# An AdaLN block with a selective scan and 16 experts on one core: ScalarE and VectorE get own moments for single stages

## The reference, cut to what matters

```
h = layernorm(x) * (1 + ca) + sa                      # ca, sa ... : one set of six vectors per row
x = x + ga * ssm(h)
h = layernorm(x) * (1 + cb) + sb
x = x + gb * moe(h)

ssm(x): xn = norm(x); xb, z = split(xn @ W_in)        # 512 channels each
        xb = silu(conv3(xb)); dt = softplus(xb @ W_dt + b_dt)
        B, C = xb @ W_B, xb @ W_C                     # 16 states
        h_t = exp(dt_t * A) * h_(t-1) + dt_t * x_t * B_t ; y_t = sum_n h_t C_t   # scan over the tokens
        y = (y + D * xb) * silu(z) ; return x + y @ W_out
moe(x): scores = sigmoid(x @ gate.T); choose 2 of 4 groups, then 4 of 16 experts; weights normalised
        y = sum_e weight_e * down_e(silu(gate_e x) * up_e x)                     # all 16 are computed
```

## Time and profile before

| | |
|---|---|
| median of three runs | 2831.57 us |
| profiled execution | 2827.36 us, its span 2825.6 us |
| busy | PE 85%, PEld 60%, DVE 86%, ACT 55%, POOL 79% |
| mean granted TensorE clock | 0.926 of full |
| DMA moved | 626.19 MB, mean 222 GB/s |

### The profile page before, as it was taken

The page is one execution under the profiler, slowest core; times in us unless marked ns, Lnnn a source line. Parts: engine busy times, 40 slices in busy tenths (PEclk is TensorE's granted clock), DMA queues, the critical chain, the costliest instruction groups (busy, mean ns, idle before and its releaser), DMA issues.

```text
span 2825.6 us, 29196 instructions
## 1 busy us (share of the span) xinstructions
PE 2398.6 (85%) x9004; PEld 1685.0 (60%) x9004; DVE 2430.4 (86%) x2482; ACT 1564.0 (55%) x2945; POOL 2237.5 (79%) x1563
## 2 busy tenths in 40 slices
PE   3445698989989898997989899898989989898899
PEld 1212466666756666675666667566666756666678
DVE  2678899989989898999989899998989899898932
ACT  3555665556556556656665665566566556655311
POOL 1577888888888888888888888888888888887922
PEclk7667899999989899999999899998989999899999
DMA  4699899999999999999999999999999999998921
GB/s 111 180 225 232 227 235 242 231 235 237 239 234 231 234 228 237 236 239 234 236 241 232 232 238 235 234 234 234 238 232 235 237 233 237 231 241 220 258 70 49
DMA packets 354510, 626.19 MB, mean 222 GB/s; under 512 B 51488, under 2 KB 162080, under 8 KB 354352
## 3 DMA queue, kind: packets, MB, share of 16 engines
q0 software_dynamic: 72960, 243.30, 45.3%
q1 hardware_dynamic: 281392, 381.01, 42.9%
HBM read 379.25 MB, written 10.06 MB: 138 GB/s over the span
## 4 chain that ended last, share of the span: by engine, by line
PE 40%; DVE 23%; issue 12%; POOL 9%; ACT 8%; DMA 7%; SPq 1%; DVEq 0%; POOLq 0%; ACTq 0%
DVE hbank L700 13%; PE wbank L477 13%; PE mbank L489 6%; PE wbank L419 4%; PE wbank L379 4%; POOL unit L1167 4%; PE wbank L505 4%; PE wbank L367 3%; DMA w_all<-w_scratch 2%; DMA w_scratch<-rows_out 2%; PE wbank L502 2%; DMA gsum<-unit 2%; DVE unit L714 2%; ACT z L823 2%; DVE act L678 2%
## 5 line engine op out<-in xcount | busy, mean ns | idle before, releaser
L1167 POOL TENSOR_TENSOR unit<-dtx,b_bc 128x1024 f32<-128x1024 f32 x512 | 1358.7, 2663 | 10.5 <-DMA b_bc<-bc_scratch 6.3
L700 DVE TENSOR_TENSOR_SCAN hbank<-hbank,unit 128x1024 f32<-128x1024 f32 x512 | 1173.3, 2292 | 103.3 <-ACT hbank L997 94.4
L997 ACT ACTIVATE hbank<-dt,a_neg 128x512 f32<-128x512 f32 x1024 | 669.2, 681 | 332.7 <-DVE unit L714 298.8
L489 PE MATMUL mbank<-down_t,act 128*128 128x256 f32 x2048 | 536.1, 402 | 57.1 <-POOL act L1135 31.2
L1179 POOL DMA_DIRECT2D gsum<-unit x448 | 452.7, 1010 | 161.4 <-DVE unit L714 75.4
L714 DVE TENSOR_TENSOR unit<-hbank,c_bc 128x1024 f32<-128x1024 f32 x448 | 545.8, 1218 | 22.3 <-DMA c_bc<-bc_scratch 1.4
L1135 POOL TENSOR_TENSOR act<-act,w_all 128x512 f32<-128x512 f32 x256 | 360.0, 1406 | 252.2 <-DVE act L678 228.2
L477 PE MATMUL wbank<-h_t,gate_t 128*128 128x256 f32 x2048 | 496.3, 386 | 24.1 <-DVE act L678 12.7
L489 PEld LDWEIGHTS mbank<-down_t,act 128*128 128x128 f32 x2048 | 402.1, 200 | 162.2 <-issue 62.6
L477 PE MATMUL wbank<-h_t,up_t 128*128 128x256 f32 x2048 | 486.9, 381 | 12.9 <-DVE gz L587 11.2
L477 PEld LDWEIGHTS wbank<-h_t,gate_t 128*128 128x128 f32 x2048 | 387.7, 192 | 128.6 <-DVE act L678 27.1
(11 more groups left out here) (122 smaller groups left out, 2400.9 us busy)
## 6 DMA issues: line engine op xcount, KB each, us to landing
gsum<-unit POOLq DMA_DIRECT2D x448, 512.0 KB, 7.5
b_bc<-bc_scratch SPq DMA_DIRECT2D x512, 256.0 KB, 6.3
c_bc<-bc_scratch SPq DMA_DIRECT2D x512, 256.0 KB, 5.5
w_all<-w_scratch SPq DMA_DIRECT2D x256, 256.0 KB, 5.0
ht<-in_L_attn_x_dram SPq DMA_DIRECT2D x16, 512.0 KB, 8.5
w_out<-in_L_attn_W_out_dram SPq DMA_DIRECT2D x16, 512.0 KB, 10.1
ht<-in_L_attn_x_dram POOLq DMA_DIRECT2D x16, 512.0 KB, 10.2
out_dram<-xt SPq DMA_DIRECT2D x16, 512.0 KB, 3.3
```

The costliest lines, as they stand in the source:

```text
L489: m = eng.matmul(mbank[:, u * H:(u + 1) * H], act[:, (n - 1) % MOE_RING, j, u * P:(u + 1) * P], down_t[:, e, :], start=(e == 0 and u == 0) ...
L700: eng.tensor_tensor_scan(h, h, unit[:, g % RING, :, :].rearrange("p a t -> p (a t)"), 0.0, ALU.mult, ALU.add).then_inc(scanned, 1)
L997: eng.activation(hbank[g % HB][:, a, :], dt[:, 2 * q + a, :], ACT.Exp, scale=a_neg[:, 2 * q + a, n:n + 1]).then_inc(decayed, 1)
L1167: eng.tensor_tensor(unit[:, g % RING, :, :], dtx[:, 2 * q:2 * q + 2, :], b_bc[:, s:s + 1, :].to_broadcast([P, 2, T]), ALU.mult).then_inc(d ...
```

## The change

It edits only the table of moments and how it is called. `streams` takes a third argument, `late`, that shifts single stages on one engine. VectorE takes mix1 one moment earlier; ScalarE takes project two moments later and silu_last and rows_bc one later. For all engines some windows move: stats, weigh, gates, silu_last, scale_wo and the loads of w_out and of both gains. SyncE runs the experts' loads and the row's output store one moment later (`W_LAG` 4 where it was `SP_LAG` 3). For the tail the experts of the last row and project, turn and pick get other moments. No instruction is added or removed.

```diff
-    LAST_EXPERTS_AT = (33, 134)
+    LAST_EXPERTS_AT = (35, 139)
...
+    W_LAG = 4
+    ACT_LATE = {"project": 2, "stats": 0, "turn": 0, "gates": 0, "silu_first": 0, "silu_last": 1, "rows_bc": 1,
+                "step_sizes0": 0, "step_sizes1": 0, "turn_in": 0, "norms": 0, "weigh": 0}
+    DVE_LATE = {"gates": 0, "silu_first": 0, "silu_last": 0, "mix0": 0, "mix1": -1, "pick": 0}
...
-        def streams(slot, stage):
+        def streams(slot, stage, late):
...
-                plan += [("mix1", behind, 4, 11, 14), ("load_gb", behind, 1, 54, 56),
-                         ("project", behind, 4, 15, 24), ("stats", behind, 5, 20, 26),
-                         ("turn", behind, 4, 27, 30), ("pick", behind, 5, 30, 32), ("weigh", behind, 2, 36, 37)]
-            plan += [("step_sizes1", slot, 9, 1, 7), ("load_wo", slot, 1, 24, 30), ("load_ga", slot, 1, 23, 26), ("scale_wo", slot, 1, 47, 47),
-                     ("scale_h", slot, 2, 56, 58), ("gates", slot, 9, 36, 42),
+                plan += [("mix1", behind, 4, 11, 14), ("load_gb", behind, 1, 56, 58),
+                         ("project", behind, 4, 15, 24), ("stats", behind, 5, 22, 26),
+                         ("turn", behind, 4, 27, 30), ("pick", behind, 5, 30, 32), ("weigh", behind, 2, 34, 36)]
+            plan += [("step_sizes1", slot, 9, 1, 7), ("load_wo", slot, 1, 33, 42), ("load_ga", slot, 1, 31, 46), ("scale_wo", slot, 1, 48, 48),
+                     ("scale_h", slot, 2, 56, 58), ("gates", slot, 9, 35, 41),
...
-                         ("silu_first", coming, 6, 57, 60), ("silu_last", coming, 6, 61, 65),
+                         ("silu_first", coming, 6, 57, 60), ("silu_last", coming, 6, 61, 66),
...
-            return [Steps(stage[name](row), n, first, final) for name, row, n, first, final in plan if name in stage]
+            return [Steps(stage[name](row), n, first + late.get(name, 0), final + late.get(name, 0))
+                    for name, row, n, first, final in plan if name in stage]
...
-            plan = [("mix1", last, 4, 5, 5), ("project", last, 4, 6, 6),
-                    ("stats", last, 5, 6, 8), ("turn", last, 4, 16, 18), ("load_gb", last, 1, 21, 26),
-                    ("pick", last, 5, 16, 16), ("weigh", last, 2, 24, 25)]
+            plan = [("mix1", last, 4, 5, 5), ("project", last, 4, 7, 7),
+                    ("stats", last, 5, 6, 8), ("turn", last, 4, 16, 17), ("load_gb", last, 1, 21, 26),
+                    ("pick", last, 5, 18, 18), ("weigh", last, 2, 24, 25)]
...
-                    experts_at(older, young, moment - SP_LAG)
+                    experts_at(older, young, moment - W_LAG)
```

More of the change, by code:

```diff
@@ L533, in _ @@
                 run = slot < NB
-                beside = streams(slot, stage_of) if run else last_streams(stage_of)
+                beside = streams(slot, stage_of, {}) if run else last_streams(stage_of)
                 young = experts_of(slot - 1, experts) if run else Halves(
@@ L781, in _ @@
                 run = slot < NB
-                beside = streams(slot, stage_of) if run else last_streams(stage_of)
+                beside = streams(slot, stage_of, DVE_LATE) if run else last_streams(stage_of)
                 young = experts_of(slot - 1, experts) if run else Halves(
@@ L1038, in _ @@
                 run = slot < NB
-                beside = streams(slot, stage_of) if run else last_streams(stage_of)
+                beside = streams(slot, stage_of, ACT_LATE) if run else last_streams(stage_of)
                 young = experts_of(slot - 1, experts) if run else Halves(
@@ L1372, in _ @@
                     load_cols(slot - 1)
-                beside = streams(slot, stage_of)
+                beside = streams(slot, stage_of, {})
                 young = experts_of(slot - 1, experts)
```

## The result

The changed kernel takes 2839.32 us (median of 12 runs, 2829.5 to 2850.95) against 2829.95 us for the kernel before (12 runs beside it, 2823.09 to 2836.82): ratio 1.0033, 95% interval 1.002 to 1.0046. It is slower by a third of a per cent, where 2825 us was forecast, with a chance of 0.17 for slower by more than 0.3%. The profiled execution took 2841.23 us (span 2839.5) against 2827.36 us; its granted clock is higher, 0.94 against 0.926.

What follows compares the result with a forecast made beforehand. No engine alone bounds the kernel, but a path of waits through each slot. Terms of -13.5, +14, -3, -4.5 and +0.5 give -6.5 us: 2825 us against the 2831.57 median, range 2804 to 2842.

Steps and rivals of the forecast that it cites:

- the part taken as nothing: Small edits priced at 0, among them experts' loads one moment later, w_out and gain loads, silu_last and rows_bc.
- term 2: Weigh and gates one moment earlier: q1's tanh delays ScalarE's apply 1.9 us, the 0.94 us weights wait goes; net +14 us.
- Term 1: Project later on ScalarE, stats later: variance, apply and TensorE's turn come 0.9 us sooner per slot; -13.5 us.
- Term 3: VectorE's mix1 one moment earlier: TensorE's project gains a small gap of weight loads, 0.2 us a slot; -3 us.
- Term 4: TensorE's clock: a shorter wait lets some slots keep 2.4 GHz through turn, 0.9 us in five slots; -4.5 us.
- The loads of w_out and the gain: Their loads on SyncE moved to moments 45 and 49, well ahead of their user: taken as 0.
- ScalarE's silu_last and rows_bc one moment later: Both wait for TensorE or VectorE where they are: taken as 0, bounds 0 to -0.3 us a slot.
- the tail's new moments: After the last row, logits come ahead of four more products and wait for the second copy: +0.5 us.
- B: Rival: experts' weights arrive late at unit 15's product behind B and C loads, the 0.94 us gap stays; 2842 us, chance 0.15.
- A: Rival: the crossing of tanh and apply on ScalarE costs nothing, the norm's chain has slack; 2811 to 2798 us, chance 0.22.
- C: Rival: VectorE's work is the bound and its waits only move; no change, 2831 us, chance 0.14.
- D: Rival: TensorE's slow clock counts in full, 4.2 us in seven slots, 29 us together; 2800 us, chance 0.04.

Runs made afterwards that it cites:

- run 1: Changed kernel with the experts' load lag (W_LAG) back at 3, all else kept: 2809.81 us, ratio 0.9937 to the kernel before.
- run 2: Kernel before with only the experts' loads on SyncE one moment later (lag 4): 2840.36 us, ratio 1.0048.
- run 3: Changed kernel with the experts' loads of moments 85 and 91 back at the old lag: 2808.31 us; with that of 85 only: 2807.58 us.
- run 4: Changed kernel, order kept, two experts' loads (moments 86 and 92) cut to half their bytes: 2821.47 us, ratio 0.9978 to the kernel before.
- run 6: Changed kernel with W_LAG 3 and ScalarE's gates one moment later: 2789.57 us, ratio 0.9867 to the kernel before.
- run 9: Kernel before with only ScalarE's project two moments later and everyone's stats from moment 22: 2811.61 us, ratio 0.9946.
- run 8: run 1 with ScalarE's project and everyone's stats back at their old moments: 2834.44 us, ratio 1.0027 to the kernel before.
- run 5: Changed kernel with gates one moment later on ScalarE alone, so the apply precedes q1's tanh: 2805.53 us, ratio 0.9928 to the kernel before.
- run 7: Changed kernel with W_LAG 3 and weigh and gates at their old moments on every engine: 2785.11 us, ratio 0.9857 to the kernel before.
- run 10: run 6 with VectorE's mix1 back at its old moment: 2792.08 us, ratio 0.9879 to the kernel before.
- run 11: run 6 with the loads of w_out and its gain, and scale_wo, at their old moments: 2798.11 us, ratio 0.9899 to the kernel before.

## Why the prediction was wrong

The direction was wrong, by a step that stands in the part taken as nothing: "The experts' loads one moment later: each is issued when GpSimd frees a buffer and used two products on; 0." Both halves of its reason failed. The load of moment 85 is not issued when the buffer comes free, but when the pair of B and C loads that it now stands behind has left. And I asked only whether the load comes late for its own user. It does not; it flies beside GpSimd's add of unit 27, which lands 2.7 us later, and what waits is the add of unit 29 and GpSimd's work behind it. Runs 1, 2 and 3 give the size, 27 us in the changed kernel and 14 alone; run 4 shows that its bytes do most of it. Run 2 shows besides that this lag, and not weigh's earlier moment, closed the gap of 0.94 us that the prediction booked under term 2: with weigh earlier and the lag at 3 (run 6) the weights' store is as late as before, 6.6 us after `w_tok`'s transpose. With that term the sum of -6.5 us would have been some +7 to +20; it came out at +9.4.

- Term 1: the mechanism was right, and every sign of it is in the trace after: no wait at the scan, the variance directly behind the drive. The turn's wait was to be 1.8 us and is 1.50. By the scans it is worth somewhat more than the 0.9 us a slot forecast: the eleventh scan comes 1.2 us sooner in run 9 than in the kernel before, and 1.2 us sooner in run 1 than in run 8 if the third scan's 0.15 is taken off.
- Term 2: the mechanism was right in each step. The multiply was to come 1.9 us later after `w_tok` and comes 1.95 later in the mean; the 0.94 us for the weights are gone; two L925 lie ahead of the apply; the scan behind the second apply was to lose 1.0 us and loses 0.95. In time the crossing alone (run 5, the gap stays closed) costs 30 us, and 1.9 us in 14 slots were 27. Where the gap comes back with its removal, runs 6 and 7 against run 1 give 20 and 23 us for the net 14. What comes on top is behind that scan. In the changed kernel the stretch from the twentieth to the twenty-first scan takes 8.6 us instead of 7.2 in 9 of 13 slots, where it did in 2 before. In those of them that were looked at, slots 3 to 14, and in no others, TensorE's clock drops to 1.2 GHz shortly before (in slot 4 the eight products L483 at 827.49 take 3.45 us behind a wait of 1.06, where the eight at 833.59 take 1.89), and VectorE then stands 1.84 us at L565 instead of 0.57. I had followed the delay only to the next wait of VectorE and called it settled there.
- Term 3: -3 us, not told from nothing (run 10).
- Term 4: too small, and no run separates it from term 1. Together they were -18 us and are -25 by run 8, -13 to -15 by run 9. By the places of run 8 the clock is 1.5 us in each of four slots between turn and gates, 6 us, and some 5 us more at the twenty-first scan, which the term did not have; it was put at 4.5. In the kernel before, the seven slots with the long slow stretch take 13.74 us from the eleventh to the thirteenth scan and the other five 12.71; slot 7, from which the rows were taken, is one of the five, so the slots do not look alike there. I had bounded the gain by the difference of whole slots, in which a slow clock's loss is mixed with what other waits take up.
- The loads of w_out and the gain: taken as 0, are worth -9 us by run 11, barely told from 0 and with an open cause.
- ScalarE's silu_last and rows_bc one moment later, and the tail's new moments, were not tested by themselves. VectorE's waits for decays fell by 1.1 us a slot in all (52.6 to 41.6 in ten), which is what term 1 takes off, so nothing points at a gain there; the tail is 0.2 us longer.
- The rivals: B was slower because experts' loads stand behind B and C loads that wait for VectorE. That is how the load of moment 86 came to leave late, and its 2842 is near the result, but its place was wrong. At L1141 of unit 15 nothing waits. That the number was near is luck. A and C are excluded by run 5 (the crossing costs) and by run 9. D, the slow clock counted in full, is too high: it gave -29 us for seven slots, 4.2 us each, and the slots with the long slow stretch are 1.0 us (before) to 1.5 us (run 8) longer at the thirteenth scan. The Trainium skill (TensorE: Matmul & The Clock Gate, HAM oscillation — how this bites in real kernels) counts half of the throttled time as lost. In run 8 the four slow slots are at 1.2 GHz for 16 us in the mean and the other eight for 7, so by that rule they would lose some 4.5 us, an estimate; the trace does not agree for the kernel's time, which shows 1.5.
- Two of the signs that were to show me wrong did: slots longer than 164.5 us (164.70), and waits that change where nothing was moved.

The parts, each as it was measured by taking it out, nearly add up. From the kernel before: terms 1 and 4 -25, term 3 -3, small loads -9, make -37 us, and run 7, which has these and the untested small edits, is at -40 (ratio 0.9857). Add term 2's 23 and the load's 27 and it is +13; the change measures +9. But a part's worth depends on the kernel it stands in: terms 1 and 4 bring 13 to 15 us in the kernel before (run 9), and with that value the sum for run 7 misses by 13; the load costs 14 us there (run 2) for 27. So the sum is a check of the size, not a proof.

## What to carry to other kernels

When a DMA is moved, list what else is in flight where it now lands, and price the slowest waiting user of those transfers, not only its own user. A queue whose head waits sets the order and the time of all behind it, so moving one load by one place can shift it by the length of a wait (here 4 us) into traffic that it had missed. And changes of an order are best tried one at a time: here a gain of 15 to 25 us hid behind two losses of 27 and 20 to 30. Last, a step that is both a loss and a gain at different places (the load lag) shows its net alone in the time; the starts of one repeated instruction, subtracted between two traces, show both.

## What the runs showed of the hardware

- The landing of a 512 KB accumulating DMA from GpSimd's queue depends on what else is in flight: 5.7 us in the mean with a 256 KB load of another queue issued 5.6 us ahead of it, 8.4 us with that load 1.6 us ahead, 7.2 us with half of that load's bytes. I had not expected 2.7 us for 256 KB. The add before it, which the load no longer flies beside, went from 6.3 to 5.0 us: the traffic moved its cost from a transfer that nobody waits for to one that holds an engine.
- The same wait of TensorE was followed by either clock. Behind 2.72 us ahead of the turn, run 8 stayed at 1.2 GHz for 13.7 to 17.1 us on end in four of twelve slots and for 7 to 10 us in eight; behind 1.50 us, run 1 stayed there for at most 7.
- A short dip has a fixed price at one place. In all fourteen traces the stretch from the twentieth to the twenty-first scan takes over 8 us in 74 of the 168 slots 3 to 14, and in exactly these the granted clock from the nineteenth scan to 4 us behind the twentieth is 0.77 to 0.79; in the other 94 it is 1.00. That the dip is the cause is argued from this match and from the order of the lines.
- The mean clock of the whole execution rose from 0.926 to 0.94 while the kernel became slower: here the clock of a profile did not tell the time by itself.
